# A fused attention and deformable convolution kernel: transposes one unit later, four normalisations split two and two, half of the row hats made one image later

## The reference

```python
x = x + attention(_gn(x), w_qkv, w_out, b_out)
x = x + deform_bn_gelu(_gn(x), proj_w, proj_b, off_w, off_b, mask_w, mask_b, gamma, beta)
```

## Time and profile before

| | |
|---|---|
| median of three runs | 3851.39 us |
| profiled execution, its span | 3848.88 us, 3847.1 us |
| first unit of image 8, of image 9 | 1007.38 us, 1117.18 us |
| one image | 109.80 us |
| TensorE busy, VectorE, ScalarE, GpSimd | 90%, 65%, 55%, 37% of the span |
| TensorE's granted clock, mean | 0.965; 1.00 inside images 1 to 30 |

### The profile page before, as it was taken

One profiled execution on the slowest core, in us unless ns is written; L12 is line 12 of the kernel. 1 busy time (PEld: TensorE's weight loads), 2 busy tenths in 40 slices (PEclk: granted clock), 3 DMA queues, 4 the chain that ended last, 5 costly groups with the idle time before them and its releaser, 6 DMA issues.

```text
span 3847.1 us, 108166 instructions
## 1 busy us (share of the span) xinstructions
PE 3470.6 (90%) x38307; PEld 3045.9 (79%) x38307; DVE 2512.4 (65%) x5517; ACT 2100.3 (55%) x4790; POOL 1429.4 (37%) x1225
## 2 busy tenths in 40 slices
PE   3899999999999999999999999999999999999500
PEld 1688888888888888888888888888888888888500
DVE  3567766666667666666677666666776666666422
ACT  1455555565565555655655556556555565555332
POOL 1344443333443433334434333344343333344211
PEclk8999999999999999999999999999999999999755
DMA  3001111111011111110111111101111111011498
GB/s 82 20 29 47 47 39 47 47 40 36 29 47 47 39 47 47 40 36 28 47 47 39 47 47 40 37 28 47 47 39 47 47 40 36 28 47 36 139 362 294
DMA packets 103965, 225.01 MB, mean 58 GB/s; under 512 B 38336, under 2 KB 64128, under 8 KB 103424
## 3 DMA queue, kind: packets, MB, share of 16 engines
q1 hardware_dynamic: 92832, 191.76, 15.8%
q0 software_dynamic: 7168, 25.17, 1.7%
q10 hardware_dynamic: 3424, 0.90, 0.1%
HBM read 87.29 MB, written 75.50 MB: 42 GB/s over the span
## 4 chain that ended last, share of the span: by engine, by line
PE 81%; issue 5%; DMA 4%; ACT 4%; DVE 3%; ACTq 1%; SPq 1%; POOL 0%; DVEq 0%; POOLq 0%
PE sps L734 12%; PE acc L751 9%; PE acc L753 9%; PE acc L752 9%; PE l L664 5%; PE zps L724 4%; PE zps L720 4%; PE zps L723 4%; PE zps L721 4%; PE zps L722 4%; DMA xn<-x_scratch 3%; PE l L596 2%; DMA out<-x 1%; PE l L595 1%; PE l L608 1%
## 5 line engine op out<-in xcount | busy, mean ns | idle before, releaser
L1368 POOL TENSOR_TENSOR sT<-ay,bx 128x768 f32<-128x768 f32 x768 | 1141.0, 1495 | 1488.4 <-PE sps L734 1480.8
L751 PE MATMUL acc<-zh,sh 128*128 128x192 f16 x4608 | 1134.1, 246 | 34.7 <-ACT ypm L968 34.7
L1179 DVE TENSOR_TENSOR sl<-sps,sh 128x384 f16<-128x384 f32 x1536 | 849.0, 553 | 478.5 <-ACT sh L947 456.6
L753 PE MATMUL acc<-zh,sl 128*128 128x192 f16 x4608 | 1133.6, 246 | 0.0
L752 PE MATMUL acc<-zl,sh 128*128 128x192 f16 x4608 | 1133.5, 246 | 0.0
L947 ACT CAST sh<-sps 128x384 f16<-128x384 f32 x1536 | 740.1, 482 | 526.0 <-PE sps L734 516.6
L923 ACT CAST zh<-zps 128x288 f16<-128x288 f32 x1536 | 618.2, 403 | 722.6 <-PE zps L724 704.3
L1173 DVE TENSOR_TENSOR zl<-zps,zh 128x288 f16<-128x288 f32 x1536 | 695.7, 453 | 380.6 <-ACT zh L923 374.3
L734 PE MATMUL sps<-eye,sT 128*128 128x128 f32 x4608 | 769.2, 276 | 4.7 <-DVE sl L1179 4.3
L734 PEld LDWEIGHTS sps<-eye,sT 128*128 128x128 f32 x4608 | 546.8, 141 | 85.5 <-issue 32.8
L751 PEld LDWEIGHTS acc<-zh,sh 128*128 128x128 f16 x4608 | 450.7, 98 | 49.3 <-ACT ypm L968 44.0
(11 more groups left out here) (176 smaller groups left out, 5243.2 us busy)
## 6 DMA issues: line engine op xcount, KB each, us to landing
x2s<-x SPq DMA_DIRECT2D x192, 255.8 KB, 2.4
xin<-in_x SPq DMA_DIRECT2D x32, 512.0 KB, 5.3
xin<-in_x SPq DMA_DIRECT2D x64, 256.0 KB, 5.7
x_scratch<-x SPq DMA_DIRECT2D x32, 512.0 KB, 2.9
y_scratch<-ych SPq DMA_DIRECT2D x32, 512.0 KB, 3.4
zh<-y_scratch SPq DMA_DIRECT2D x20, 512.0 KB, 10.9
zl<-x_scratch SPq DMA_DIRECT2D x20, 512.0 KB, 12.4
out<-zh POOLq DMA_DIRECT2D x20, 512.0 KB, 9.2
```

What stands on the lines that cost most here:

```text
L751: pe.matmul(acc[:, 0:C], s_h, zh[:, j, ky, z], start=start and kx == 0, stop=False)
L753: mm = pe.matmul(acc[:, 0:C], s_l, zh[:, j, ky, z], start=False, stop=stop and kx == 2)
L1179: dve.tensor_tensor(one(sl), sps[u % 2][:, 0:3 * P], one(sh), ALU.subtract).then_inc(s_lo, 1)
L1368: pool.tensor_tensor(sT[:, p % ST_RING].rearrange("p k (r x) -> p k r x", r=R), a, x_, ALU.mult)\
```

## The change

Five things are altered, and every instruction that ran before still runs.

- `turn_x0` to `turn_x3` go from units 6 to 9 to units 7 to 10, and the attention behind them, `apply` and the moments of its result one unit on too. `group1` goes from 24 to 25, `rstd1` from 25 to 26, where `norm4` stays.
- `norm6` and `norm7` go from units 28 and 30 to units 30 and 31, `low6` and `low7` from 31 and 32 to 32 and 33. `norm4`, `norm5`, `low4`, `low5` and `edges` stay.
- The second half of the row hats, which was made for the next image in units 44 to 46, is made inside the image that uses it: distances in unit 8, ScalarE's part in unit 11, the rest in unit 12. `column_hats1` goes from unit 46 to 44, and column quarter 2 from ScalarE's unit 14 to 16.
- `turn_y(1)` goes from unit 25 to 26; `scale_y(0)` and `scale_y(1)` from 16 and 26 to 17 and 27.
- The two `y_stats` of the image before go from units 7 and 8 to 9 and 10.

```diff
         PLAN = {-10: ("x_stats0", "x_stats1"), -9: ("x_stats2", "x_stats3"), -6: ("moments0",), -3: ("group0",),
                 0: ("rstd0", "norm0"), 1: ("norm1",), 2: ("norm2", "low0"), 3: ("norm3", "low1"),
-                4: ("low2",), 5: ("low3",), 6: ("turn_x0",), 7: ("turn_x1",), 8: ("turn_x2",), 9: ("turn_x3",),
...
+                4: ("low2",), 5: ("low3",), 7: ("turn_x0",), 8: ("turn_x1",), 9: ("turn_x2",), 10: ("turn_x3",),
...
-        TURN_Y, SCALE_Y = (14, 25, 36), (16, 26, 37)
+        TURN_Y, SCALE_Y = (14, 26, 36), (17, 27, 37)
+        ROWS_1 = (8, 11, 12)
...
                     elif left:
                         split_s(u + 2 - UNITS, b + 1)
-                    if u in (14, 24):
-                        column_hats((14, 24).index(u) + 2, b, par)
+                    if u in (16, 24):
+                        column_hats((16, 24).index(u) + 2, b, par)
+                    if u == ROWS_1[1]:
+                        row_act(1, b, par)
...
-                    if u in (7, 8) and i is None and not first(b):
-                        y_stats(u - 5, b - 1, 1 - par)
+                    if u in (9, 10) and i is None and not first(b):
+                        y_stats(u - 7, b - 1, 1 - par)
                     if u in (33, 34) and i is None:
                         y_stats(u - 33, b, par)
+                    if u == ROWS_1[0]:
+                        row_distance(1, b, par)
+                    if u == ROWS_1[2]:
+                        row_hats(1, b, par)
```

More of the change, by code:

```diff
@@ L901, in part0, with row_act @@
                 if name == "row_act":
[L902 to L907, removed]
+                    row_act(q, b, par)
                 if name == "column_hats":
                     column_hats(q, b, par)
+            def row_act(h, b, par):
+                d = ay_half(h, par).rearrange("p t k n -> p (t k n)")
+                act.wait_ge(dy_sb, 2 * b + h + 1)
+                act.activation(d, d, ACT.Abs)
+                act.drain()
+                act.activation(d, d, ACT.Relu, scale=-1.0, bias=1.0).then_inc(hat_act, 1)
             def column_hats(q, b, par):
@@ L1137, in part0, with row_distance, row_hats @@
                 if name == "rows":
[L1138 to L1142, removed]
-                if name == "row_hats":
[L1144 to L1152, removed]
+                    row_distance(q, b, par)
+                if name == "row_hats":
+                    row_hats(q, b, par)
+            def row_distance(h, b, par):
+                dve.wait_ge(off_sb, b + 1)
+                dve.tensor_tensor(ay_half(h, par), spread(off[:, par, half_tiles(h, par), 0:TAPS], R),
+                                  cy_sb[:, None, None, 0:R].broadcast_to([P, TILES // 2, TAPS, R]), ALU.add)\
+                   .then_inc(dy_sb, 1)
+            def row_hats(h, b, par):
+                dve.wait_ge(hat_act, 2 * b + h + 1)
+                tiles = half_tiles(h, par)
+                zero_outside(ay[:, par], NEAR_ROWS, [t for t in (0, TILES - 1) if tiles.start <= t < tiles.stop])
+                if h == 0:
+                    dve.tensor_scalar(mask[:, par], mask[:, par], 1.0, None, ALU.add)
+                dve.drain()
+                dve.tensor_tensor(ay_half(h, par), ay_half(h, par), spread(mask[:, par, tiles], R), ALU.mult)\
+                   .then_inc(hats, 1)
             def offset_distance(b, par):
```

## The result

The changed kernel takes 3820.9 us, the median of five runs (3810.4 to 3829.7). Beside it the kernel before took 3850.8 (3847.0 to 3856.2). The ratio is 0.9923, with a 95% interval of 0.9901 to 0.9944. That is 29.6 us off, where 54.7 were forecast. The profiled execution took 3820.0 us, of which its trace spans 3818.2, against 3847.1 before.

What follows compares the result with a forecast made beforehand. TensorE, busy for 90% of the span, was taken as the bound, leaving its waits to win. Stalls 73.4 plus small terms 0.5 less late copies 19.2 gave 54.7 us off, about 3796 us; range 3772 to 3823.

Steps and rivals of the forecast that it cites:

- the three stalls: TensorE waits in unit 6 for `low3`, in units 30 and 0 for ScalarE's copy; all go, 73.4 us together.
- The copy in unit 30: First product of unit 30 waits for ScalarE's copy of `acc` behind `norm6`; 0.74 us in 31 images, 22.9 gained.
- The copy at the image's end: First product of the next image's unit 0 waits for ScalarE's copy behind the column hats; 31 x 0.68, 21.1 gained.
- the slower case: Rival: in unit 26 ScalarE waits at `norm4` for `nbias`, TensorE behind it; 3882 us at 3.5 of waiting; chance 0.05.
- a sign of being wrong: Three signs: ScalarE waits for `nbias` in unit 26, unit 38 waits over 1.6 us, or the image stays near 109.
- the new wait: Unit 38's z piece waits behind `edges` in about half the images, 1.24 us late each; 19.2 us lost.
- units with slack: Moved `turn_y(1)`, `scale_y` and `y_stats` pass units with slack; counted among small terms that come to 0.5 gained.
- how many images are late: Copies of the shifted planes: half the images in time to within 0.1, half 1.24 late; 15.5 x 1.24 = 19.2 us lost.
- none late: Rival: the copies of the shifted planes are in time in every image; 3777 us; chance 0.18.
- all late: Rival: the copies of the shifted planes are late in every image; 3815 us, up to 3827; chance 0.14.
- image 0's squeezed table: In image 0 the moved stages round to other units; costed at 0 within 2 us either way.
- a stall that stays: Rival: one of the three stalls stays, `low3` slipping or ScalarE still behind at a copy; about 3821 us; chance 0.09.

Runs made afterwards that it cites:

- The first experiment: Changed kernel with an image's first two `y_stats` in VectorE's units 30 and 31 instead of 33 and 34; 3802.3 us, ratio 0.9860 to the kernel before.
- The last experiment: Changed kernel with `norm6`, `norm7`, `low6`, `low7` one unit earlier, plus image 0's old squeezed table for the moved stages; 3771.4 us, ratio 0.9799 to the kernel before.

## Why the prediction was right on the three stalls, missed one cost and mis-sized another

**Right: the three stalls.** Each went whole, and each has its own measured price now. `turn_x0`: forecast 29.4, measured 27.1. The copy in unit 30: 22.9 and 21.8. The copy at the image's end: 21.1 and 20.2. The sum is 69.1 against 73.4. In images 1 to 30 of the profiled executions the three cost 29.2, 20.8 and 22.2 us. Image 0 gave back 2.7 and 2.8 in the first and the last, where TensorE was at 1.2 GHz for 3.4 us of it and not for 10.2.

**Right: what `turn_x0` and the copies meet next.** Nothing took the place of those stalls in their own units. The wait of ScalarE for `nbias` in unit 26, on which the slower case rested, came in 14 images, at 0.3 us each. The prediction named such a wait as a sign of being wrong. It also held that ScalarE can be some 0.7 late before TensorE feels it, and in these images TensorE waits there for nothing.

**Right: where the new wait would be.** `low7` ends 9.58 us after the start of unit 30 instead of 7.33, so 2.25 later; 2.2 was forecast. Unit 38 waits for `edges`, 1.5 us in image 9 and 1.24 was forecast for a late one.

**Wrong: that `y_stats` goes past units with slack.** I followed `y_stats` in front of `low7` only for what it does to `low7`. `low6`, slowed by GpSimd, then `y_stats` and `low7` are 2.4 us of VectorE's work beside its two residues for each unit. The residue behind them is late for unit 35. The sum had 0 there, and it cost 16.1 us with image 0. The first experiment took `y_stats` out and got 15.5 back in images 1 to 30. This is over half of the error, and the rows of before had all of its durations.

**Wrong in size: how many images are late.** I took half, since before the change half the images had a packet among the copies: every even image but the last, and no odd one. After it 13 of the 15 even ones had one still, and 10 of the 15 odd ones as well, since the copies, 2.2 us later, came to where the other packets were. The cost was 26.8 us instead of 19.2. Unit 35 works the other way: it makes TensorE ask 0.51 later, and the mean wait is 1.17 instead of 1.24. I had named both outcomes as rivals, none late and all late, and the truth lies nearer the second. The packets cost the copies 1.0 to 1.9 us, and with all packets moved clear of them the copies took 4.10 to 4.15 us in 30 of 30 images. The Trainium skill, "Runtime: NRT & Kernel Launch", section "Instruction fetch mechanics", calls the crossing of a 16 KiB block mostly hidden. That is said of the engine's own instructions; for these copies the runs show the 1.0 to 1.9 us.

**Wrong, small: image 0 and the beginning.** For image 0's squeezed table I had 0 within 2. It puts `gram_wq0` and `logits0` into one unit, 14, and costs 3.5 (image 0 is 2.6 longer, though its two copies no longer wait, 1.5, and 0.6 of it is unit 35). The last experiment shows that the old placing avoids the loss, and by the estimate made there nearly all of it is what the clock cost, 3.4 us. Ahead of image 0 I had 1 gained, and 0.8 was lost.

The failures come to 16.1 + 7.6 + 3.5 + 1.8 = 29.0 us. Small gains that I had not counted, 1.4 of them in image 29, take 3.2 off. That leaves 25.8, and the spans differ by 54.7 - 28.9 = 25.8 as well.

**In part luck: the range.** The time came out inside the range that I gave, 2 us below its upper end, and just over half of the forecast gain came. The upper end, 3823, was there for a stall that stays, and none stayed. The cost of unit 35 was in no rival. One more of my signs of being wrong came true: the image is still near 109, 108.8 on average.

## What to carry to other kernels

When operations are moved on an in-order engine, add up all that the engine does in the units around the new place, and compare the end of every item behind it with the moment at which its reader asks; following only the moved item misses who stands behind it. Where a short chain of DMAs has to land by a moment, plan it by its slowest case: a shift by one row of the table was the difference between 0.2 us left in the worst image and 1.5 us lost. And take a change of several parts apart on the chip: two of these three gave all of the gain, and the third alone made the kernel slower until it stood one unit earlier.

## What the runs showed of the hardware

- A 16 KB packet of the instruction queue (335 packets are 5.49 MB in the changed kernel) among four DMAs from SBUF to SBUF, two of 256 KB and two of 72 KB, delays their landing: 5.1 to 6.0 us instead of 4.12, though the queue has 0.8% of the DMA engines' time in that stretch. That fits with an instruction packet going ahead of or between theirs on an engine that they share; which engine it was, and how they are ordered there, was not measured.
- The place of these packets depends on the length of TensorE's program ahead of the loop. 52 transposes that run once changed 23 late images into none, and brought a stop of 1.1 to 2.1 us at the end of the loop's body instead, 13 times. The cause of that stop stays open.
- The changed kernel's runs spread over 19 us, those of the one with the normalisations a unit earlier over 7. Late copies are not needed for such a spread: with the row hats back no image waits for them, and the runs spread over 15 us. The cause stays open.
- TensorE's granted clock fell in one stretch of image 0, from 1.00 in the kernel before to a mean of 0.80 to 0.87 over 20 us, when one table of that image replaced another. It is at 1.00 there again with the old table.
